# Integer feed-forward: rows' norm and rounding on GpSimd, residual one tile later

## The reference, cut

```
def _act_quant(x):
    scale = 127.0 / jnp.clip(jnp.max(jnp.abs(x), axis=-1, keepdims=True), 1e-05)
    xq = jnp.clip(jnp.round(x * scale), -128.0, 127.0) / scale
...
gate = jax.nn.silu(_bitlinear(x, w_gate))        # 256 -> 1024
up = _bitlinear(x, w_up)                         # 256 -> 1024
return _bitlinear(gate * up, w_down)             # 1024 -> 256
...
x = x + _L1_ffn_ref(_layernorm(x, axis=-1), ...)
```

## Time and profile before

| | us |
|---|---|
| median of 3 runs | 3317.25 (3316.61 to 3318.8) |
| the profiled execution | 3315.08 |
| its span | 3313.3 |
| busy in the span: TensorE, VectorE, ScalarE, GpSimd | 3080.8, 2349.5, 1097.8, 939.7 |

### The profile page before, as it was taken

The page is one execution under the profiler, slowest core; times in us unless marked ns, Lnnn a source line. Parts: engine busy times, 40 slices in busy tenths (PEclk is TensorE's granted clock), DMA queues, the critical chain, the costliest instruction groups (busy, mean ns, idle before and its releaser), DMA issues. The chain is left out here.

```text
span 3313.3 us, 63191 instructions
## 1 busy us (share of the span) xinstructions
PE 3080.8 (93%) x25558; PEld 2280.3 (69%) x25558; DVE 2349.5 (71%) x6201; ACT 1097.8 (33%) x1925; POOL 939.7 (28%) x1001
## 2 busy tenths in 40 slices
PE   5999899899599988798999999999999978998999
PEld 3777666566367755576788888888888855776544
DVE  5778355200277779765898999999899865777666
ACT  3444311122145669754222222222222204444000
POOL 2333000133233410000345345345345433332000
PEclk9999999899799999998999999999999978999999
DMA  4100220144401000302000000000000002000000
GB/s 131 36 32 2 74 73 14 31 116 120 140 16 39 15 12 1 127 26 86 3 6 4 4 6 4 5 6 4 4 6 4 5 7 87 27 27 2 13 19 20
DMA packets 82688, 112.16 MB, mean 34 GB/s; under 512 B 12256, under 2 KB 62688, under 8 KB 82016
## 3 DMA queue, kind: packets, MB, share of 16 engines
q1 hardware_dynamic: 76256, 99.60, 9.1%
q0 software_dynamic: 6144, 8.52, 1.4%
HBM read 87.00 MB, written 21.10 MB: 33 GB/s over the span
## 5 line engine op out<-in xcount | busy, mean ns | idle before, releaser
L2022 POOL TENSOR_TENSOR pk_hisig<-pk_hihot,pk_sigs 128x512 f16<-128x512 f16 x512 | 520.3, 1043 | 666.2 <-DVE pk_hihot L2296 664.7
L2119 PE MATMUL pk_ps<-X,ew_downT 128*128 128x256 f32 x2048 | 480.8, 386 | 0.0
L2165 PE MATMUL pk_ps<-ew_up,pk_act_h 128*128 128x256 f32 x2048 | 461.5, 384 | 1.7 <-DVE pk_act_h L2284 1.7
L2165 PEld LDWEIGHTS pk_ps<-ew_up,pk_act_h 128*128 128x128 f32 x2048 | 391.3, 192 | 56.9 <-issue 2.0
L2119 PEld LDWEIGHTS pk_ps<-X,ew_downT 128*128 128x128 f32 x2048 | 382.0, 192 | 59.4 <-issue 14.8
L2030 ACT ACTIVATE pk_act_h<-pk_ps 128x512 f32<-128x512 f32 x256 | 152.8, 597 | 546.8 <-PE pk_ps L2119 546.8
L2297 DVE TENSOR_TENSOR pk_lohot<-pk_iota_h,pk_ps 128x1024 f16<-128x1024 f16 x256 | 311.4, 1217 | 0.0
L580 DVE RECIPROCAL a_rden<-a_ps_o 128x256 f32<-128x256 f32 x96 | 168.3, 1754 | 158.3 <-PE a_ps_o L465 158.2
L569 DVE TENSOR_REDUCE a_mx<-a_ps_s 128x8 f32<-128x1024 f32 x192 | 226.0, 1219 | 54.3 <-PE a_ps_s L439 54.1
L273 ACT ACTIVATE a_pT<-a_ps_t 128x512 f32<-128x512 f32 x384 | 208.7, 598 | 142.4 <-PE a_ps_t L448 142.3
L2489 PE MATMUL mo_ps<-mw_we,mo_xnT 128*128 128x512 f32 x512 | 225.5, 599 | 0.0
(11 more groups left out here) (352 smaller groups left out, 5233.5 us busy)
## 6 DMA issues: line engine op xcount, KB each, us to landing
ro_w<-in_L_W SPq DMA_DIRECT2D x16, 1024.0 KB, 7.7
a_ctx_t<-in_ctxT SPq DMA_DIRECT2D x24, 512.0 KB, 3.9
a_tau<-in_tau SPq DMA_DIRECT2D x24, 256.0 KB, 4.1
a_delta<-in_delta SPq DMA_DIRECT2D x24, 256.0 KB, 4.4
X<-in_x SPq DMA_DIRECT2D x4, 1024.0 KB, 9.7
row_dram<-sh_row SPq DMA_DIRECT2D x8, 512.0 KB, 3.0
sum_dram<-sh_new SPq DMA_DIRECT2D x8, 512.0 KB, 2.9
X<-sum_dram SPq DMA_DIRECT2D x4, 1024.0 KB, 9.4
```

The source lines that it names most:

```text
L2022: ins = pool.tensor_tensor(hisig[:, buf, n, :, :, :], hi, sig2.broadcast_to([P, TP, 2, ECH]), ALU.mult)
L2119: ins = pe.matmul(hid.bank(f"h{c}")[:, j * 2 * P:(j + 1) * 2 * P], downT[:, k, e * P:(e + 1) * P], XT[:, p, k, :], start=(k == 0), stop=(k ...
L2165: ins = pe.matmul(tail.bank("y")[:, 0:D], act_h[:, p % 2, c, s * P:(s + 1) * P], up[:, c, :], start=(c == 0), stop=(c == ECH - 1))
```

## The change

Norm and `x_rounded` become GpSimd instructions. GpSimd does norm 0 and 1, rounds x of tiles 0 and 1, and from then on norm t and `x_rounded` t in turn; norm t waits until TensorE has transposed tile t-2, whose buffer it takes. `asc_ready` now counts the two factors of the start too, so ScalarE waits for t+3. VectorE no longer waits for its reciprocal ahead of `dequants`, and does `finish(t-2)` behind the products of turn t, where it did `finish(t-1)` at the turn's end; the last two are done behind the loop.

```
--- before.py
+++ after.py
@@ -1381,10 +1381,6 @@
 
         @block.scalar
         def _(act):
-            def norm(t):
-                act.activation(xn[:, t % 2, :], X[:, t, :], ACT.Identity, scale=rstd[:, t:t + 1],
-                               bias=nmr[:, t:t + 1]).then_inc(xn_ready, 1)
-
             def x_columns(t):
                 xt.wait_full(act, t, "xt")
                 xt.take(act.activation(xqT[:, t % 2, :, :], xt.bank("xt")[:, 0:D].rearrange("p (k n) -> p k n", k=KC),
@@ -1398,7 +1394,7 @@
                                            scale=dq[:, t % 2, 0:1]), f"g{n}")
 
             def h_rounded(t):
-                act.wait_ge(asc_ready, t + 1)
+                act.wait_ge(asc_ready, t + 3)
                 act.activation(hr[:, :], h[:, t % 2, :], ACT.Identity, scale=asc[:, t % 2, 1:2],
                                bias=shift[:, 0:1]).then_inc(hr_ready, 1)
 
@@ -1409,22 +1405,38 @@
                         "p (k n) -> p k n", k=4), ACT.Identity, bias=shift[:, 1:2]), f"ht{n}")
 
             act.activation(rstd[:, :], MV[:, :, 1], ACT.Sqrt, bias=keep["eps"][:, 0:1]).then_inc(rstd_sq, 1)
-            act.wait_ge(nmr_ready, 1)
-            norm(0)
-            norm(1)
             x_columns(0)
             gates(0)
             x_columns(1)
-            norm(2)
             for t in range(TILES):
                 if t + 1 < TILES:
                     gates(t + 1)
                 h_rounded(t)
                 if t + 2 < TILES:
                     x_columns(t + 2)
-                if t + 3 < TILES:
-                    norm(t + 3)
                 h_columns(t)
+
+        @block.gpsimd
+        def _(pool):
+            def norm(t):
+                if t >= 2:
+                    xt.wait_full(pool, t - 2, "xt")
+                pool.tensor_scalar(xn[:, t % 2, :], X[:, t, :], rstd[:, t:t + 1], nmr[:, t:t + 1], ALU.mult,
+                                   ALU.add).then_inc(xn_ready, 1)
+
+            def x_rounded(t):
+                pool.wait_ge(asc_ready, t + 1)
+                pool.tensor_scalar(xn[:, t % 2, :], xn[:, t % 2, :], asc[:, t % 2, 0:1], ROUND, ALU.mult,
+                                   ALU.add).then_inc(xr_ready, 1)
+
+            pool.wait_ge(nmr_ready, 1)
+            norm(0)
+            norm(1)
+            x_rounded(0)
+            x_rounded(1)
+            for t in range(2, TILES):
+                norm(t)
+                x_rounded(t)
 
         @block.tensor
         def _(pe):
@@ -1496,10 +1508,6 @@
                 inc(dve.tensor_scalar(amx[:, s, at], amx[:, s, at], 1e-5, 1.0 / 127.0, ALU.max, ALU.mult))
                 return dve.reciprocal(asc[:, s, at], amx[:, s, at])
 
-            def x_rounded(t):
-                dve.tensor_scalar(xn[:, t % 2, :], xn[:, t % 2, :], asc[:, t % 2, 0:1], ROUND, ALU.mult,
-                                  ALU.add).then_inc(xr_ready, 1)
-
             def dequants(s):
                 return dve.tensor_tensor(dq[:, s, :].rearrange("p (a b) -> p a b", a=2),
                                          wmean[:, :].rearrange("p (a b) -> p a b", a=2),
@@ -1514,8 +1522,7 @@
             for t in range(2):
                 dve.wait_ge(xn_ready, t + 1)
                 step(largest(xn[:, t, :], t, 0))
-                step(factors(t, slice(0, 1), step))
-                x_rounded(t)
+                factors(t, slice(0, 1), step).then_inc(asc_ready, 1)
                 dequants(t).then_inc(dq_ready, 1)
             dve.wait_ge(dq_ready, 2)
 
@@ -1543,6 +1550,8 @@
                                                      dq[:, s, 1:2], gt[:, s, n * 512:(n + 1) * 512], ALU.mult,
                                                      ALU.mult), f"u{n}")
                 dve.wait_ge(dq_ready, t + 2)
+                if t >= 2:
+                    finish(t - 2)
                 if more:
                     dve.wait_ge(xn_ready, t + 3)
                     link.inc(largest(xn[:, s, :], s, 0))
@@ -1559,16 +1568,12 @@
                     link.wait(dve)
 
                 factors(s, slice(0, 2), scaled).then_inc(asc_ready, 1)
-                dve.wait_ge(asc_ready, t + 1)
-                if more:
-                    x_rounded(t + 2)
                 dequants(s).then_inc(dq_ready, 1)
-                if t >= 1:
-                    finish(t - 1)
                 link.close()
 
             dve.wait_ge(dq_ready, TILES + 2)
-            finish(TILES - 1)
+            for t in (TILES - 2, TILES - 1):
+                finish(t)
 
 
 WINDOW = 16.0
```

## The result

| | before | after |
|---|---|---|
| median, us | 3318.16 of 5 runs (3316.61 to 3318.8) | 3300.38 of 5 runs (3299.3 to 3302.16) |
| ratio | | 0.9949, interval 0.9934 to 0.9963 |
| the profiled execution, its span | 3315.08, 3313.3 | 3301.98, 3300.2 |

The kernel is faster, by 17.8 us between the medians. The two profiled executions differ by 13.1 us. The ratio's interval leaves out 1, so the sign is clear of noise; how much of the 17.8 us is the change's own is less so, and the last group of experiments goes into it.

What follows compares the result with a forecast made beforehand. VectorE was taken to bound the kernel at 4.72 us a tile, falling to 4.34. 28 tiles save 11.2 us and the end 1.25, 12.4 in all: 3317.25 - 12.4 = 3304.8 us, range 3302 to 3310.5.

Steps and rivals of the forecast that it cites:

- Part 1: `x_rounded` leaves VectorE and `dequants` follows the reciprocal without a wait: 0.38 us a tile saved, bounds 0.27 to 0.39.
- Part 4: GpSimd does norm and rounding, about 0.56 us each, in time for TensorE and VectorE and without slowing VectorE.
- The last two tiles: End of the stage: VectorE also skips the reduction of x, 4.01 us each, 8.0 for 9.29, 1.25 saved.
- The loop through ScalarE and TensorE: From one rounding of h through transposes, `hqT` and gates to the next: 4.27 us, just under VectorE's 4.34.
- the old place of `finish`: Right behind `dequants`, L1525 would wait 0.6 us for TensorE's sums; behind the products, 1.32 us of work covers that.
- Rivals 2, 3 and 4: GpSimd late (3311.5, chance 0.08); `dequants` held by GpSimd (3325, 0.08); nothing happens, saved time returns as waits (3317, 0.02).
- rival 2: GpSimd is late: beyond 0.8 us an instruction, each 0.1 lengthens the loop by 0.1; 3311.5 at 1.1; chance 0.08.
- rival 3: `dequants`, with two SBUF operands, is held until GpSimd's `x_rounded` is done: tile 5.06 us, total 3325; chance 0.08.
- VectorE's tile: VectorE's time per tile falls from 4.72 by 0.38 to 4.34 us and stays the bound by 0.07.
- rival 1: The loop through ScalarE and TensorE is longer than 4.27 us: at 4.45 the gain is 9 us, 3308; chance 0.08.
- the fill: Start of the stage: two GpSimd instructions cost +0.3 us, faster first tiles give about 0.3 back; sum zero.
- the first tiles' gain in full: First tiles no longer wait for ScalarE's norm and run at 4.27 us until VectorE is behind: about 0.3 back.

Runs made afterwards that it cites:

- finish_only: The kernel before with only `finish` of tile t-2 moved behind the products; x rounded on VectorE, norm on ScalarE: median 3312.93 us, ratio 0.9986.
- h_split: The changed kernel with the rounding of h in two halves, so TensorE can begin with the first: median 3300.35 us, ratio 0.9941.
- finish_old: The changed kernel with `finish` of tile t-1 back at the turn's end, behind `dequants`: median 3314.41 us, ratio 0.9993.
- pool_twice: The changed kernel with one more GpSimd instruction of 0.48 us ahead of each `x_rounded`: 3300.24 us in one run.
- two_inputs_beside: The changed kernel with an extra VectorE instruction (128x4, both operands in SBUF) between the two products, while GpSimd does norm: 3302.58 us in one run.
- before_again: The kernel before run once more with no edit: median 3317.07 us of 11 runs, ratio 0.9999.

## Why the prediction was right, and where it was wrong

**Right.** Part 1: `dequants` follows the reciprocal's start by 0.08 (0.09 forecast). From finish_only (4.680) to h_split (4.285), where in both VectorE is the bound, the rounding's leaving is worth 0.395 us a tile; I had 0.38, with 0.39 as the upper bound. Part 4: GpSimd's two instructions take 479 and 549 ns, inside 0.40 to 0.735, and cost nothing; VectorE is not slowed (products 746 ns beside GpSimd, 743 without it in finish_only). The last two tiles: 1.27 for 1.25, but that is luck: I had two tiles of 4.01, and they took 4.30 and 3.73, the first still held by the loop through ScalarE and TensorE. The loop through ScalarE and TensorE: 4.30 for 4.27, all its legs a hundredth or two longer, the rounding of h itself 1254 ns for 1242. The size of the wait that the old place of `finish` would have: 0.6 forecast, 0.68 in finish_old. Rivals 2, 3 and 4 did not come: pool_twice shows the cover of rival 2. Two things speak against rival 3: `dequants` starts 0.08 behind the reciprocal, ahead of GpSimd, and in two_inputs_beside a VectorE instruction of its size that comes second is held up by 0.03 us and no more.

**Wrong in size, first term: VectorE's tile.** The step was "nothing is saved on VectorE" by the move of `finish`, and with it "VectorE's tile becomes 4.72 - 0.38 = 4.34 us". finish_only shows the move to save 0.04 by itself, and the leaving of `x_rounded` saved 0.395: 4.285. The bound therefore went to the ScalarE loop at 4.30, not to VectorE at 4.34, and "VectorE stays the bound by 0.07" is false; rival 1's mechanism (the loop as the bound) is what happened, at 4.30 and not at 4.45. For the time that is 28 x 0.04 = 1.1 us more gain; with 0.2 in the fill, which I had set at zero, and hundredths elsewhere it makes the stage's 13.8 for 12.4.

**Wrong, second step: from the profiled execution to the median.** I set the median of after 2.17 us above its profiled execution, as it stood in the runs of before, and "nothing outside the stage moves". Against the profiled execution alone the forecast was 3302.7, and 3301.98 was measured: 1.4 too high for the stage, 0.7 too low for the rest. But after's median stood 1.6 below its profile, where before's stood 2.2 to 3.1 above its own. That profile of before was one of the minority with clock 0.970 (9 of 84 executions, where 54 have 0.969), and its stage ended at the full clock, which is worth about 1 us of the 3; what the rest of the step hides stays open. Of the 4.4 us between 3304.8 and 3300.38, 1.4 are the stage and 3.0 are this step. The range had no term for it: its lower end came from the stage alone (3302 with the first tiles' gain in full), and a us or two of scatter of a median, and the 2.17 taken off, would have put it near 3299.

**What I had priced rightly without knowing how much hung on it.** The wait of 0.6 that the new place of `finish` avoids was written as the price of a detail. finish_old shows it to be the whole gain: a wait of 0.68 in every second tile costs 0.76 a pair on VectorE, and 0.38 a tile is all that part 1 brings.

## What to carry to other kernels

When an instruction leaves the engine that bounds a loop, the others come due earlier by the same amount: look for the operand on that engine whose producer does not move (here the sums, 4.88 us after the rounding of h), and move its reader, or nothing is won. Work that is taken from an engine with slack, like norm here, is worth nothing until that engine's loop is the bound. Where limits lie close together, here 4.30 and 4.285 us with a third at 4.075, a forecast is good to their distance only; and a forecast made from one profiled execution needs a term of its own for how that execution stood to the median, here 2 to 3 us of 3300.

## What the runs showed of the hardware that I had not expected

- GpSimd's norm of 128x256, already running for 0.08 us, is stretched from 0.55 to 0.84 us by a VectorE instruction with two SBUF operands that takes 0.41; VectorE's own takes 415 ns in the median and is hardly touched. With four numbers a row on VectorE the contest costs one of the two 0.03 us.
- GpSimd's `tensor_scalar` of 128x256 is cheap: 479 ns with one factor per row and a constant, 549 with two numbers per row, against 735 for the addition of two tensors of that size.
- The mean granted TensorE clock of an execution differs between 0.968 and 0.972 with no change of the kernel, and 0.969 in place of 0.970 goes with 3.8 us in before.
- Behind a wait of 2.06 us at the end of a stage that had run at the granted clock of 1.00, TensorE's eight transposes took 1.66 to 1.97 us for 1.09 in five of six profiles, at the lower level of 1.2 GHz in before_again; behind a wait of 1.09 they took 1.09 in all six.
